# Three narrow-head attentions: where the strip copies, the turns and the output projection stand in the engines' orders

## Time and profile before

| | |
|---|---|
| median of 3 runs | 2508.88 us (2505.51 to 2517.94) |
| the profiled execution's own time | 2485.77 us |
| its span, first to last instruction | 2483.6 us |
| mean granted TensorE clock | 0.952 |
| TensorE, VectorE, ScalarE, GpSimd busy | 88%, 61%, 45%, 30% |
| L1 attention, gated attention, L3 attention | about 229, 248 and 280 us of the span |

### The profile page before, as it was taken

The page is one execution under the profiler, slowest core; times in us unless marked ns, Lnnn a source line. Parts: engine busy times, 40 slices in busy tenths (PEclk is TensorE's granted clock), DMA queues, the critical chain, the costliest instruction groups (busy, mean ns, idle before and its releaser), DMA issues. The chain is left out here.

```text
span 2483.6 us, 38366 instructions
## 1 busy us (share of the span) xinstructions
PE 2174.7 (88%) x10438; PEld 1376.0 (55%) x10486; DVE 1512.0 (61%) x3702; ACT 1125.3 (45%) x3555; POOL 745.6 (30%) x932
## 2 busy tenths in 40 slices
PE   6969999988888688879999999999995788869999
PEld 3446677756455344435556656665653444445685
DVE  6975434456455577765676777677765577753244
ACT  2021244411455355545565556555552477742242
POOL 5705500056233200023344444344433100003104
PEclk9969999999999899999999999999997699979999
DMA  6902245453200000000000000000000000201143
GB/s 218 300 21 85 91 136 161 147 163 114 118 1 0 3 1 0 0 26 1 1 1 1 0 0 0 0 0 0 0 0 1 5 5 4 84 24 42 61 134 100
DMA packets 85587, 127.18 MB, mean 51 GB/s; under 512 B 12418, under 2 KB 74626, under 8 KB 84226
## 3 DMA queue, kind: packets, MB, share of 16 engines
q1 hardware_dynamic: 75490, 98.52, 12.5%
q0 software_dynamic: 9984, 27.28, 3.5%
HBM read 91.41 MB, written 47.84 MB: 56 GB/s over the span
## 5 line engine op out<-in xcount | busy, mean ns | idle before, releaser
L2371 ACT ACTIVATE l2x_prob<-l2x_pS,l2x_nb,l2x_rms_q 128x256 f32<-128x256 f32 x256 | 142.5, 565 | 116.5 <-DVE l2x_nb L2606 114.7
L1035 ACT ACTIVATE moe_act_g<-moe_pG 128x96 f32<-128x96 f32 (+1 forms) x159 | 53.2, 335 | 267.2 <-PE moe_pU L968 186.9
L1186 PE MATMUL l2x_pQ<-big,l2x_xT 128*128 128x512 f32 x312 | 149.6, 602 | 4.7 <-DVE l2x_part L2584 4.3
L2603 DVE TENSOR_REDUCE l2x_negmax<-l2x_pS 128x2 f32<-128x512 f32 x128 | 87.7, 685 | 92.5 <-PE l2x_pS L2191 89.7
L928 POOL DMA_INDIRECT moe_yk<-route_y,moe_slot_i x72 | 71.1, 987 | 218.9 <-DMA route_y<-moe_y 188.5
L3113 DVE TENSOR_TENSOR l3f_hid<-l3f_act_g,l3f_pA 128x256 f32<-128x256 f32 (+1 forms) x103 | 38.1, 370 | 159.0 <-ACT l3f_act_g L3024 117.6
L2201 PE MATMUL l2x_pOT<-l2x_probT,l2x_v 128*128 128x512 f32 x256 | 124.7, 610 | 4.5 <-ACT l2x_probT L2386 4.5
L2191 PE MATMUL l2x_pS<-l2x_kT,l2x_qT 128*128 128x256 f32 x512 | 128.3, 380 | 0.0
L2937 PE MATMUL l3f_pA<-big,l3f_xnT 128*128 128x512 f32 x256 | 125.4, 614 | 0.0
L2210 PE MATMUL l2x_pT<-big,l2x_oT 128*128 128x256 f32 x512 | 121.1, 379 | 0.7 <-ACT l2x_oT L2379 0.7
L1515 ACT ACTIVATE l1f_ex<-l1f_pS,l1f_negmax 128x128 f32<-128x128 f32 x256 | 73.0, 368 | 104.0 <-DVE l1f_negmax L1546 104.0
(11 more groups left out here) (498 smaller groups left out, 5753.1 us busy)
## 6 DMA issues: line engine op xcount, KB each, us to landing
route_x<-in_c_zero SPq DMA_DIRECT2D x1, 13184.0 KB, 81.6
moe_xg<-route_x SPq DMA_DIRECT2D x103, 128.0 KB, 2.2
route_y<-moe_y SPq DMA_DIRECT2D x103, 128.0 KB, 1.7
big<-in_e_gu SPq DMA_DIRECT2D x1, 6144.0 KB, 19.0
l3f_xg<-route_x SPq DMA_DIRECT2D x39, 128.0 KB, 2.2
route_y<-l3f_y SPq DMA_DIRECT2D x39, 128.0 KB, 1.7
big<-in_f_gu SPq DMA_DIRECT2D x1, 4096.0 KB, 12.2
big<-in_e_down SPq DMA_DIRECT2D x1, 3072.0 KB, 25.0
```

Of the source, the lines that this page charges most:

```text
L1186: last = pe.matmul(out, lhsT=xT[:, k, :], rhs=w[:, k, cols], start=(k == 0), stop=(k == KC - 1))
L2371: ins = act.activation(prob[g % 2][:, h, :], pS[j][:, (h % 2) * 2 * P:(h % 2 + 1) * 2 * P], ACT.Exp, scale=rms_q[g][:, h:h + 1], bias=nb[: ...
L2603: dve.tensor_reduce(negmax[:, c], pS[j][:].rearrange("p (h k) -> p h k", h=2), AX.X, ALU.max, negate=True).then_inc(S["max_steps"], 1)
```

## The change

The same instructions run in other places. In the L1 attention `spread` follows `turn`, ahead of `xT`, `attT` and S3; `out` becomes a step of lag 4 behind S0; S2 goes before `normalise` and `zed`; the turned result uses the bank of the turned keys. ScalarE gets an order of its own, in which `attT` stands before S3. In the gated attention S2 goes before `rows`, S3 before `ternary`, and on TensorE S3 before `turn` and `back`. In the L3 attention `spread` follows `quantX` and stands before S3, `out` goes ahead of `xq` and uses the bank of the turned queries. `Turned` counts its whole copy in a new semaphore `whole_read`, on which the new users of the banks wait.

```diff
--- before.py
+++ after.py
@@ -1130,7 +1130,7 @@
     def __init__(self, ph, G, ps_q, ps_k, k_tiles=4, spread="k"):
         self.G, self.ps_q, self.ps_k, self.kt, self.spread = G, ps_q, ps_k, k_tiles, spread
         self.rows_ready, self.turned_ps, self.ready = (ph.sem(n) for n in ("rows_ready", "turned_ps", "qk_ready"))
-        self.blank = ph.sem("blank")
+        self.blank, self.whole_read = ph.sem("blank"), ph.sem("whole_read")
         self.q = ph.sb("q_rows", [P, NH, SLOT])
         self.k = ph.sb("k_rows", [P, 4 * k_tiles, SLOT])
         if spread == "k":
@@ -1165,7 +1165,7 @@
             act.wait_ge(self.blank, 2)
         k, q = self.ps_k[:, 0:self.kt * P], self.ps_q[:, 0:4 * P]
         whole, parts = (q, k) if self.spread == "k" else (k, q)
-        act.activation(self.plain[p][:].rearrange("p m t -> p (m t)"), whole, ACT.Copy)
+        act.activation(self.plain[p][:].rearrange("p m t -> p (m t)"), whole, ACT.Copy).then_inc(self.whole_read, 1)
         self.strip(act, p, parts, 0)
         self.strip(act, p, parts, 1)
 
@@ -1222,10 +1222,11 @@
                                 "pv_done", "oT_ready", "back_ps", "den_steps", "att_ready", "attT_ps", "attT_ready", "out_ps", "delta_ready",
                                 "stats1", "stats2", "rstd2", "zed_ready", "tail_pool"))
         v_clear = ph.sem("v_clear")
-        order = (("S0", 2), ("stats", 0), ("qk", 1), ("V3", 3), ("oT", 3),
-                 ("S1", 2), ("v", 1), ("V0", 2), ("rows", 1), ("normalise", 0), ("zed", 4),
-                 ("S2", 2), ("back", 3), ("xT", 0), ("divide", 3), ("V1", 2), ("turn", 1),
-                 ("attT", 3), ("S3", 2), ("V2", 2), ("spread", 1), ("out", 3))
+        first_half = (("S0", 2), ("out", 4), ("stats", 0), ("qk", 1), ("V3", 3), ("oT", 3),
+                      ("S1", 2), ("v", 1), ("V0", 2), ("rows", 1), ("S2", 2), ("normalise", 0), ("zed", 4),
+                      ("turn", 1), ("back", 3), ("divide", 3), ("V1", 2), ("spread", 1), ("xT", 0))
+        order = first_half + (("S3", 2), ("attT", 3), ("V2", 2))
+        act_order = first_half + (("attT", 3), ("S3", 2))
         block = ph.block()
 
         @block.sync
@@ -1276,9 +1277,9 @@
         def _(pe):
             pe.wait_ge(*G["loaded"]["small"])
 
-            def xT(b, p):
-                after(pe, attT_ready, b - 3)
-                nm.tensor(pe, b, p)
+            def turn_rows(b, p):
+                after(pe, attT_ready, b - 2)
+                tq.tensor(pe, b)
 
             def queries_keys(b, p):
                 pe.wait_ge(nm.xT_ready, b + 1)
@@ -1319,10 +1320,9 @@
 
             def turn_out(b, p):
                 pe.wait_ge(att_ready, b + 1)
-
-                pe.wait_ge(nm.xT_ready, min(b + 4, B) if isinstance(b, int) else b + 4)
+                pe.wait_ge(tq.whole_read, min(b + 3, B) if isinstance(b, int) else b + 3)
                 for k in range(KC):
-                    last = pe.transpose(pT[:, C + k * P:C + (k + 1) * P], att[:, k * P:(k + 1) * P], G["ident"][:])
+                    last = pe.transpose(pTk[:, k * P:(k + 1) * P], att[:, k * P:(k + 1) * P], G["ident"][:])
                 last.then_inc(attT_ps, 1)
 
             def out(b, p):
@@ -1330,7 +1330,7 @@
                 pe.wait_ge(v_ready, min(b + 3, B) if isinstance(b, int) else b + 3)
                 project(pe, pV[:, C:2 * C], attT, W["L1_xattn_Wo"]).then_inc(out_ps, 1)
 
-            steps = {"xT": xT, "qk": queries_keys, "v": value_rows, "turn": lambda b, p: tq.tensor(pe, b),
+            steps = {"xT": lambda b, p: nm.tensor(pe, b, p), "qk": queries_keys, "v": value_rows, "turn": turn_rows,
                      "back": back, "attT": turn_out, "out": out}
             for s in range(4):
                 steps[f"S{s}"] = lambda b, p, s=s: scores(b, p, s)
@@ -1348,7 +1348,7 @@
             def turn_out(b, p):
                 act.wait_ge(attT_ps, b + 1)
                 after(act, out_ps, b)
-                act.activation(attT[:].rearrange("p k t -> p (k t)"), pT[:, C:2 * C],
+                act.activation(attT[:].rearrange("p k t -> p (k t)"), pTk[:, 0:C],
                                ACT.Copy).then_inc(attT_ready, 1)
 
             def o_turned(b, p):
@@ -1360,7 +1360,7 @@
                      "spread": lambda b, p: tq.scalar_rest(act, b, p), "attT": turn_out, "oT": o_turned}
             for s in range(4):
                 steps[f"S{s}"] = lambda b, p, s=s: exp(b, p, s)
-            pipeline(act, order, steps, peel=6)
+            pipeline(act, act_order, steps, peel=6)
 
         @block.vector
         def _(dve):
@@ -1592,10 +1592,12 @@
         v_clear = vs_clear
         sm = HeadSoftmax(ph, G, tq, pS, pP, pO, pQK, G["identb"], lambda p: causal[:].rearrange("p m t -> p (m t)"),
                          lambda p, h: vs[p][:], lambda p, m: tq.blocks[p][:, 0, :, :])
-        order = (("S0", 2), ("P3", 3), ("stats", 0), ("V2", 3), ("qkv", 1),
-                 ("S1", 2), ("P0", 2), ("V3", 3), ("oT", 3), ("pick", 1), ("rows", 1),
-                 ("S2", 2), ("P1", 2), ("V0", 2), ("turn", 1), ("back", 3), ("normalise", 0), ("ternary", 1),
-                 ("S3", 2), ("P2", 2), ("V1", 2), ("xT", 0), ("divide", 3))
+        first_half = (("S0", 2), ("P3", 3), ("stats", 0), ("V2", 3), ("qkv", 1),
+                      ("S1", 2), ("P0", 2), ("V3", 3), ("oT", 3), ("pick", 1), ("S2", 2), ("rows", 1),
+                      ("P1", 2), ("V0", 2))
+        pe_order = first_half + (("S3", 2), ("turn", 1), ("back", 3), ("P2", 2), ("V1", 2), ("xT", 0))
+        order = first_half + (("turn", 1), ("normalise", 0), ("S3", 2), ("ternary", 1), ("P2", 2), ("xT", 0),
+                              ("divide", 3))
         ternary = Ternary(ph, G, pO)
         block = ph.block()
 
@@ -1652,7 +1654,7 @@
                     pe.wait_ge(ternary.sum_steps, 7)
                 sm.values(pe, b, p, 0)
 
-            pipeline(pe, order, {"xT": xT, "qkv": qkv, "back": lambda b, p: sm.back(pe, b, qkv_read),
+            pipeline(pe, pe_order, {"xT": xT, "qkv": qkv, "back": lambda b, p: sm.back(pe, b, qkv_read),
                                  **sm.tensor_steps(pe), "S0": first_scores, "V0": first_values})
 
         @block.scalar
@@ -1771,7 +1773,7 @@
         order = (("S0", 2), ("P3", 3), ("M0", 2), ("stats", 0), ("V2", 3), ("quantA", 4), ("qk", 1),
                  ("S1", 2), ("v", 1), ("P0", 2), ("M1", 2), ("V3", 3), ("oT", 3), ("rows", 1),
                  ("S2", 2), ("aq", 4), ("M2", 2), ("P1", 2), ("V0", 2), ("turn", 1), ("back", 3), ("normalise", 0), ("quantX", 0),
-                 ("S3", 2), ("P2", 2), ("V1", 2), ("xq", 0), ("M3", 2), ("spread", 1), ("out", 4), ("divide", 3))
+                 ("spread", 1), ("S3", 2), ("P2", 2), ("V1", 2), ("out", 4), ("xq", 0), ("M3", 2), ("divide", 3))
         block = ph.block()
 
         @block.sync
@@ -1839,7 +1841,6 @@
 
             def turn_a(b, p):
                 pe.wait_ge(qa.ready, b + 1)
-                after(pe, out_read, b)
                 pe.wait_ge(kv_read, latest(b, 4))
                 for k in range(KC):
                     last = pe.transpose(pTb[:, C + k * P:C + (k + 1) * P], qa.q[:, k * P:(k + 1) * P], G["identb"][:])
@@ -1857,10 +1858,13 @@
                 project(pe, pQK[:, 0:C], xqT, qwT["q"])
 
             def value_rows(b, p):
-                after(pe, out_read, b - 3)
                 project(pe, pT[:, C:2 * C], cT[p], W["L3_wv"]).then_inc(qkv_ps, 1)
                 if isinstance(b, int) and b == 0:
                     weights(1)
+
+            def turn_rows(b, p):
+                after(pe, out_read, b - 3)
+                tq.tensor(pe, b)
 
             def first_values(b, p):
                 if isinstance(b, int) and b == 0:
@@ -1869,12 +1873,12 @@
 
             def out(b, p):
                 pe.wait_ge(aqT_ready, b + 1)
-                pe.wait_ge(xqT_ready, latest(b, 5))
-                project(pe, pT[:, C:2 * C], aqT, qwT["o"]).then_inc(out_ps, 1)
+                pe.wait_ge(tq.whole_read, latest(b, 4))
+                project(pe, pTq[:, 0:C], aqT, qwT["o"]).then_inc(out_ps, 1)
 
             pipeline(pe, order, {**sm.tensor_steps(pe), "xq": turn_x, "aq": turn_a, "qk": queries_keys,
                                  "v": value_rows, "back": lambda b, p: sm.back(pe, b, kv_read), "out": out,
-                                 "V0": first_values},
+                                 "V0": first_values, "turn": turn_rows},
                      peel=6)
 
         @block.scalar
@@ -1967,7 +1971,7 @@
             def out(b, p):
                 dve.wait_ge(out_ps, b + 1)
                 after(dve, added, b)
-                dve.tensor_scalar(outp[:], pT[:, C:2 * C], qa.step[p][:, 0:1], None, ALU.mult).then_inc(out_read, 1)
+                dve.tensor_scalar(outp[:], pTq[:, 0:C], qa.step[p][:, 0:1], None, ALU.mult).then_inc(out_read, 1)
                 dve.wait_ge(out_read, b + 1)
                 dve.tensor_tensor(outp[:], outp[:], sw["o"][:], ALU.mult).then_inc(out_steps, 1)
```

## The result

| | before | after |
|---|---|---|
| median of 4 runs each | 2507.20 us (2503.89 to 2517.94) | 2447.41 us (2445.39 to 2452.77) |
| profiled execution, its span | 2485.77, 2483.6 | 2448.54, 2446.4 |
| ratio | | 0.9762 [0.9738, 0.9786] |

What follows compares the result with a forecast made beforehand. Each attention stage was taken as bound by a ring of waits, no engine reaching 90%. Terms -10.6 (L1), -7 (gated) and -26 (L3) sum to -43.6 us, taken off the median 2508.88: 2465 us, range 2440 to 2494.

Steps and rivals of the forecast that it cites:

- The ring of S2, clip, exp, key copy, strips and S0: L1 attention: this loop of waits sets the turn; 5.58 us from S2 to S0, new turn 11.93, gain 0.76.
- 14 turns at one gain: L1 attention: fourteen intervals between S0s each gain 0.76 us, together -10.6 us; bounds 0 and 18.
- P3 waits for the copy instead: Gated attention: P3 starts behind VectorE's copy P2 at 988.06, not behind the exp at 988.59; 0.5 us a turn, -7 us.
- VectorE is a next bound: L3 attention: VectorE binds next; its 1.41 us wait for the projection goes, 0.48 stays; turn 13.42 us.
- as the first ones hang on quantising the weights: L3 attention: only 13 turns counted, at 2.0 us each, leaving out the first ones; -26 us.
- the projection, x turn and S0 now fall into what were three almost empty microseconds, so I also count the clock drops out: L3 attention: clock drops end as an idle stretch fills; gain 2.0 us a turn against the mean of 15.43.
- Rival B: L3 attention keeps its clock drops; its part is -18 us, total 2473 us; chance 0.17.
- The rule that I had weighed: Trainium skill's rule on clock swings, for L3 attention: idles remain, so drops stay; -18 us instead of -26.
- C: A stage's gain becomes another wait, likeliest in L3; 2484 us at a quarter of its gain, 2491 at none; chance 0.19.
- E: L3, L1: late exp of S3 holds P3 and V3 if L3's S0 gains under 1.2 us; slower, 2532 us; chance 0.07.
- D: All stages: the places taken are as late as those left, no gain; 2509 us; chance 0.09.
- the route through the median: Whole program: the sum of -43.6 us taken off the median 2508.88, not the profiled 2485.77; 2465 instead of 2442 us.

## Why the prediction was right, and where it was off

**The L1 attention: mechanism right, -18.6 for -10.6.** The ring of S2, clip, exp, key copy, strips and S0 was the bound and is so still, with the wait of 0.87 where 0.85 was forecast. A turn gained 0.95 for the 0.76 predicted: S2 to S0 is 0.12 shorter than added up (the key copy starts 0.54 after the exp does, where 0.63 and 0.03 were counted; the four strips take 2.37, as counted), and S0 to S2 0.08, since the projection, out of its wait, adds 0.87 (6.27 against 5.40) and not 0.95. Of the 15 intervals between S0s the last thirteen gained 12.1, the first two (11.93 and 10.80 for 13.12 and 14.19) 4.6; the first S0 comes 1.3 earlier after the stage's start, and 0.6 are at the end. What was mis-sized is mainly the head: 14 turns at one gain have no place for intervals that gain 1.2 and 3.4. Some 1.7 of the 3.4 is a clock drop: the second interval has a clock of 0.88 before and 1.00 after, and in the two traces where the old order has 1.00 there it takes 12.5 (and the first interval then 14.3). The stage as a whole is steadier than its parts: 229.7 to 231.7 us in eight traces with the old order, 211.2 to 211.7 in five with the new one. The kernel with the last strips back confirms the mechanism by its size: 1.36 a turn worse.

**The gated attention: right, -7 predicted.** The step "P3 waits for the copy instead" is the row of the wait, and the gain of a turn is 0.45 (0.5 predicted). Alone it gives 5.7 us by the ratio and 4.3 by the medians. In the profiled pair it shows 3.6: fourteen intervals gained 6.4, the first lost 1.3, the first S0 comes 1.0 later and the end of the stage takes 0.5 more. That loss isn't the order's. The first interval is 13.3 in four of nine traces with the old order, at a clock of 1.00, and 15.5 to 15.8 in five, at 0.84 to 0.86; with the new one it is 12.3 at 1.00, and 14.6 and 14.7 at 0.83 to 0.84. The pair had caught the old order at 1.00 and the new one at 0.84. Like with like, the whole stage takes 240.5 for 247.5 to 247.9, and 244.2 to 244.3 for 251.0 to 251.8: a gain of some 7.2 either way, which is the forecast. Why the clock at this place differs between executions wasn't tried.

**The L3 attention: right, -34.6 for -26.** VectorE is a next bound, as said: its 1.41 is gone and its 0.48 left, and the fused multiplications show it, as far as 0.46 of 0.84 goes. The busy shares alone wouldn't, as TensorE has more (105.75 of 117.50 us for 104.73). Without drops the turn was to be 13.42; the mean is 13.06 to 13.09. The last twelve intervals gained 26.1, or 2.2 each for the 2.0 predicted, and the first three, which the forecast left out "as the first ones hang on quantising the weights", another 7.2 (40.3 for 47.5), so the order holds them too: the strips' place, which alone gave 6.8 there. This is the larger part of what was mis-sized. With the old order these first intervals also vary: in three of the other traces two or more of them took 17.0 to 17.2 and not 15.8; with the new order each is the same within 0.3 in all four traces that have this phase as changed.

**The clock.** The step "the projection, x turn and S0 now fall into what were three almost empty microseconds, so I also count the clock drops out" held: 0.94 before, 1.00 after. Rival B, with the drops kept, would have had 8 us more. The two kernels with extra matmuls show the cause by itself, as far as this: filling both waits ends the drops, filling one (the first) doesn't. The waits of TensorE at a turn's end, and the clock of the steady turns:

| kernel and stage | waits, us | clock |
|---|---|---|
| before, L3 | 1.31 and 1.32 | 0.94 |
| before with one wait filled, L3 | 0.56 and 1.32 | 0.94 |
| before with both filled, L3 | 0.57 and 0.45 | 1.00 |
| only the projection moved, L3 | 2.79 | 0.94 |
| only the strips moved, L3 | 2.20 or 2.42 | 0.95 |
| changed, L3 | 0.52 | 1.00 |
| before, L1 attention | 0.47 and 0.84 | 1.00 |
| changed, L1 attention | 0.87 | 1.00 |
| last strips back, L1 attention | 2.22 | 0.96 |

TensorE has other short waits in the middle of a turn: 0.38 in the L3 attention before and after, with 0.48 more in every second turn after, and 0.56, 0.49 and 0.43 in the gated attention before, at 1.00. At a drop the granted clock goes from its higher level (2.4 GHz) to the lower (1.2 GHz) close to the first scores behind such a wait. What separates the rows at 1.00 from the others exactly stays open: I varied the waits, not the pattern of work between them. The rule that I had weighed (the Trainium skill, TensorE: Matmul & The Clock Gate, A second HAM failure mode: psum-queue depth-cycling) says that short idles between groups of matmuls with cycled banks make the clock swing. The swing and its tie to idles agree with these traces. That section of the Trainium skill gives no size for the idles, only that they come frequently enough. I had read it as if any would do, and that reading fails, as TensorE still idles 11.75 us in nine turns of the changed L3 attention, cycles the same banks and stays at 1.00. By my reading of that rule the L3 part would have been -18; it was -34.6.

**The rivals.** C (a stage's gain turns into another wait) is what each L3 edit does alone: -2.5 and +2 us. The change escapes it because it moves both. It was possible to see that in the earlier trace rows, where the two waits of TensorE and the one of VectorE stand within 3 us, and I didn't price the halves. E (the exp of S3 late behind the strips) has the right place but not the threshold reached: S0 in L3 comes early enough that P3 starts 0.14 after the exp's end. D is excluded by each stage's own gain.

**The base.** I subtracted from the median of 2508.88 a sum worked out in an execution of 2485.77. The three stages changed by -56.8 in the profiled pair; 2508.88 less that is 2452, within 5 us of the measured 2447. With the gated stage compared at the same clock (-7.2) it is -60.4 and 2448. So the route through the median was right: by the 17.5 us found above, most of the 23 us between median and profiled execution seem to lie ahead of the three stages, where nothing was changed. That wasn't known when the difference was taken off; there it was a guess that held. The miss of 18 us is the size of two terms, 8 in the L1 attention and 8.6 in the L3 attention, both for the larger part at the head of the stage.

## What to carry to other kernels

Where a stage waits on a ring, list every wait of a turn that lies within the ring's slack and ask for each edit which of them it leaves: two edits that are worth nothing alone were worth 32 us together, and a sum over the steady turns can leave out as much again: here the first intervals of two stages gave 4.6 and 7.2 us. Look at the granted clock turn by turn when turns come in unequal lengths; short waits of TensorE that lie close together may cost more than their own length, and cutting one of them or joining two can leave the cost or bring it to a stage that had none. Compare stages by their own start and end before comparing whole spans: here the part that nobody touched differed by 17.5 us between two profiled executions. And compare stages at the same granted clock in their first turns: half of the gated stage's gain had seemed lost by that alone.

## What the runs showed of the hardware that I had not expected

The same code ahead of the L1 attention took 630.8 us in the profiled execution of the result and 611 to 617 in the thirteen others; the kernel before has a median of 2507.2 beside the result and of 2489.1 to 2489.9 on the chips of the experiments. The first interval of the gated attention took 13.3 us in some executions and 15.5 to 15.8 in others of the same instructions, with a granted clock of 1.00 or of 0.84 to 0.86. Adding four f32 matmuls a turn, each for 128x256 values, made the program 6 us faster, by holding TensorE's clock. And two strip copies put back behind three other instructions of ScalarE brought clock drops of 1.7 us in every third turn to a stage whose steady turns had shown none.
